# Four-layer decoder on one core: two stage boundaries of layer 2 interleaved, and layer-norm statistics moved

## The reference

```
x = x + tanh(g_ffn[1])   * L1_ffn(layernorm(x))        # entmax gates, two rank-64 maps, gelu
x = x + tanh(g_xattn[2]) * L2_xattn(layernorm(x), ctx)
    Sim = hc@w1 + hq@w2 + (hc*w3)@hq.T + b             # hc: tokens, hq: 64 context rows
    hq_hat = softmax(Sim, 2) @ hq
    hc_bar = softmax(max(Sim, 2), 1) @ hc              # one row for each batch of 256 tokens
    out = [hc, hq_hat, hc*hq_hat, hc*hc_bar] @ W_qv + b_qv
x = x + tanh(g_ffn[2])   * L2_ffn(layernorm(x))        # 16 experts, top 4 by sigmoid, SiLU; one shared
x = x + tanh(g_xattn[3]) * L3_xattn(layernorm(x), ctx) # 16 heads over 64 keys
x = x + tanh(g_ffn[3])   * L3_ffn(layernorm(x))        # 8 experts, top 2, with capacity
```

## Time and profile before

| | |
|---|---|
| executions shown, median | 1265.06 us |
| the profiled execution, its span | 1268.88 us, 1266.9 us |
| PE busy | 1069.6 us, 84% of the span |
| DVE busy | 762.4 us, 60% |
| ACT busy | 476.9 us, 38% |
| POOL busy | 354.3 us, 28% |
| chain that ended last | PE 58%, issue 17%, DVE 13%, ACT 5%, DMA 4% |
| mean granted TensorE clock | 0.899 |

### The profile page before, as it was taken

How to read it: one execution, slowest core, us unless ns; L and a number is a source line. 1 busy time by engine, 2 the same in 40 slices (tenths; PEclk the granted TensorE clock), 3 DMA queues, 4 the chain that set the end, 5 groups by cost and what they waited for, 6 DMA issues and landing times.

```text
span 1266.9 us, 17786 instructions
## 1 busy us (share of the span) xinstructions
PE 1069.6 (84%) x6301; PEld 649.1 (51%) x6302; DVE 762.4 (60%) x2192; ACT 476.9 (38%) x914; POOL 354.3 (28%) x391
## 2 busy tenths in 40 slices
PE   7889999987889986997988899999898883398870
PEld 5346666655534445334774566666455442166650
DVE  2667777778856677764664555556567764443324
ACT  1445555540034442552224233432344431254523
POOL 0050000001252175201325113000426554255551
PEclk9989999995579995898998999999999995599995
DMA  7091000030000002000003345333000011400016
GB/s 176 18 324 42 1 1 1 1 83 0 0 1 1 2 1 106 1 1 1 1 1 68 69 96 106 69 68 68 1 2 29 25 35 35 186 28 32 28 37 210
DMA packets 36163, 61.90 MB, mean 49 GB/s; under 512 B 5969, under 2 KB 20408, under 8 KB 34994
## 3 DMA queue, kind: packets, MB, share of 16 engines
q1 hardware_dynamic: 31474, 52.33, 15.3%
q0 software_dynamic: 4608, 8.50, 2.1%
HBM read 40.40 MB, written 21.45 MB: 49 GB/s over the span
## 4 chain that ended last, share of the span: by engine, by line
PE 58%; issue 17%; DVE 13%; ACT 5%; DMA 4%; POOL 2%; another core or an unknown queue 1%; SPq 0%; DVEq 0%; POOLq 0%; ACTq 0%
PE bank L534 6%; PE bank L412 5%; PE bank L455 5%; PE bank L1124 5%; PE bank L1065 3%; PE bank L1135 2%; PE bank L441 2%; PE bank L392 2%; PE bank L597 2%; PE bank L448 2%; PE bank L1079 2%; DVE nmax L1915 2%; DMA big_a<-gates 2%; PE bank L553 2%; ACT att L1278 2%
## 5 line engine op out<-in xcount | busy, mean ns | idle before, releaser
L1065 PE MATMUL bank<-big_b 128*128 128x512 f32 x288 | 140.4, 613 | 0.0
L1915 DVE TENSOR_REDUCE nmax<-bank 128x16 f32<-128x1024 f32 x64 | 78.4, 1225 | 62.4 <-PE bank L540 38.0
L1585 POOL TENSOR_SCALAR xn<-xw,mean,rstd 128x128 f32<-128x128 f32 x64 | 51.3, 810 | 189.1 <-PE bank L515 95.6
L1745 POOL DMA_INDIRECT expert_outs<-big_a,big_b x80 | 77.9, 974 | 76.4 <-DVE big_a L2534 54.3
L1461 ACT ACTIVATE att<-bank 128x512 f32<-128x512 f32 (+1 forms) x72 | 43.0, 597 | 141.6 <-PE bank L1065 141.2
L1079 PEld LDWEIGHTS bank<-big_b,att 128*128 128x128 f32 (+1 forms) x576 | 73.1, 192 | 33.5 <-issue 17.4
L2423 DVE TENSOR_TENSOR att<-att,bank 128x512 f32<-128x512 f32 (+1 forms) x72 | 49.2, 684 | 63.8 <-PE bank L1079 59.4
L1079 PE MATMUL bank<-big_b,att 128*128 128x128 f32 (+1 forms) x576 | 78.3, 279 | 5.8 <-DVE xw L1858 4.0
L1732 POOL DMA_INDIRECT expert_rows<-xw,big_b x64 | 63.3, 989 | 68.7 <-DVEq L2013 52.0
L1858 DVE SCALAR_TENSOR_TENSOR xw<-bank,tg,xw 128x128 f32<-128x128 f32 (+3 forms) x80 | 43.0, 537 | 65.4 <-PE bank L455 47.0
L1278 ACT ACTIVATE att<-bank 128x1024 f32<-128x1024 f32 x64 | 62.0, 1021 | 44.0 <-PE bank L576 44.0
(11 more groups left out here) (409 smaller groups left out, 2235.4 us busy)
## 6 DMA issues: line engine op xcount, KB each, us to landing
big_a<-gates SPq DMA_DIRECT2D x14, 1024.0 KB, 9.7
expert_rows<-big_b SPq DMA_DIRECT2D x1, 5240.0 KB, 20.3
expert_outs<-big_b SPq DMA_DIRECT2D x1, 4096.0 KB, 32.5
big_a<-expert_outs SPq DMA_DIRECT2D x6, 512.0 KB, 7.8
big_a<-expert_rows SPq DMA_DIRECT2D x1, 2620.0 KB, 14.4
xw<-in_x SPq DMA_DIRECT2D x1, 2048.0 KB, 11.0
big_a<-in_mask SPq DMA_DIRECT2D x2, 1024.0 KB, 12.4
big_b<-in_w_in SPq DMA_DIRECT2D x1, 2048.0 KB, 8.3
```

The source lines that it names most:

```text
L1065: mm = nc.tensor.matmul(bank[2 * (n % 3) + k][:, :], w13[:, k, c * 128:(c + 1) * 128], xnT_all[:, g * GW:(g + 1) * GW], start=True, stop=True)
L1585: ins = nc.gpsimd.tensor_scalar(xn[:, b % 2, j], x[:, t], mean[:, t:t + 1], rstd[:, t:t + 1], SUB, MUL)
L1745: nc.gpsimd.indirect_dma_start(outs3, bass.IndirectOffsetOnAxis(numbers3[:, ex, i:i + 1].bitcast(u32), 0), xs[:, ex, i, 0:D], None, bounds ...
L1915: nc.vector.tensor_reduce(nmax[:, j], psum[:, 2048:3072].rearrange("p (h t) -> p h t", t=T), AX.X, MAX, negate=True).then_inc(s.free, 1)
```

## The change

PE. The features of group 0 of the similarity attention are transposed in mumoe's last turn, and its similarities stand between the two halves of that turn's second rank map. The 12 unread matmuls are gone. Layer 3's keys and gate weights move from the experts' start into turn 0 of the similarity attention. In the attention's last turn PE also does the experts' features, logits and the first two `up`. The waits for `layer_done` 4 and 5 are gone. Here is PE at the end of mumoe before (L873, L879, L888: hidden, second rank map, outputs; L1009 the unread matmuls; L936 features, L945 and L947 similarities; L956 maxima, L980 probabilities):

```diff
@@ -900,2 +900,4 @@
             gate_transposes(g + 1)
+        else:
+            features_s(0)
         hidden(g, 1)
@@ -909,2 +911,6 @@
         rank2(g, 0)
+        if last:
+            pe.wait_ge(r_g_evac, 2 * NG - 1)
+            pe.wait_ge(m.g2, 3)
+            similarities(0)
         rank2(g, 1).then_inc(r_z2, 1)
@@ -1007,32 +1011,47 @@
-    for n in range(12):
-        nc.tensor.matmul(bank[5][:, :], identb[:, :], negI[:, :], start=True, stop=True)
...
+    def turns(features2, logits2, up2):
+        for g in range(NG):
+            if g:
+                pooled_transpose(g - 1)
+                if g == 1:
+                    pe.wait_ge(keys_evac, 6)
+                outputs_attended(g - 1)
+            maxima_transposes(g)
+            if g:
+                outputs_own(g - 1)
+            else:
+                layer3_keys(0)
+                layer3_gates()
+            probability_transposes(g)
+            if g + 1 < NG:
+                features(g + 1)
+            attended(g)
+            if g == NG - 1:
+                features2(0)
+            weight_transposes(g)
+            if g == 0:
+                layer3_keys(1)
+            pooled(g)
+            if g + 1 < NG:
+                similarities(g + 1)
+        logits2(0)
+        pooled_transpose(NG - 1)
+        outputs_attended(NG - 1)
+        pe.wait_ge(m.sub, NG)
+        up2(0)
+        outputs_own(NG - 1)
+        up2(1)
+    return features, similarities, turns
+def layer3_keys(n):
+    if n:
+        pe.wait_ge(r_o_read, NG)
+    nc.tensor.matmul(bank[(5, 7)[n]][:, :], wblk[:, 0], ctxT[:, n * 512:(n + 1) * 512],
+                     start=True, stop=True).then_inc(keys_mm, 1)
...
+def layer3_gates():
+    nc.tensor.matmul(bank[4][:, 0:NE3], y[:, 0], wg3, start=True, stop=True).then_inc(keys_mm, 1)
...
+def experts2(similarity_turns):
@@ -1082,9 +1107,7 @@
-    features(0)
-    logits(0)
-    for n in range(NC2 * NG):
+    similarity_turns(features, logits, up)
+    gate_transpose(0)
+    for n in range(2, NC2 * NG):
         g, c = divmod(n, NC2)
         up(n)
-        if n == 0:
-            gate_transpose(0)
         if g + 1 < NG:
@@ -1159,11 +1182,7 @@
 pe.wait_ge(layer_done, 3)
-mumoe()
-pe.wait_ge(layer_done, 4)
 pe.wait_ge(dma_w[1], 3 * 16)
-similarity_attention()
-pe.wait_ge(layer_done, 5)
 pe.wait_ge(dma_blk, 32)
-layer3_keys()
-pe.wait_ge(keys_evac, 7)
-down2 = experts2()
 pe.wait_ge(g_built, 2 * B)
@@ -1392,2 +1411,4 @@
                     gate_evac(g + 1)
+                else:
+                    first_similar()
         if first:
@@ -1417,9 +1438,17 @@
-def similarity_attention():
+def layer3_keys(n):
+    act.wait_ge(keys_mm, (5, 7)[n])
+    nc.scalar.activation(khat[:, n * 512:(n + 1) * 512], bank[(5, 7)[n]][:, :], ACT.Identity,
+                         bias=colb[:, COL_BK:COL_BK + 1]).then_inc(keys_evac, 1)
-    def feature_evac(g):
-        act.wait_ge(m.xT, g + 1)
-        nc.scalar.copy(xnT[:, g % 2], bank[0][:, :]).then_inc(m.xT_evac, 1)
+def layer3_gates():
+    act.wait_ge(keys_mm, 6)
+    nc.scalar.copy(wg3, bank[4][:, 0:NE3]).then_inc(keys_evac, 1)
+def similar_features(g):
+    act.wait_ge(m.xT, g + 1)
+    nc.scalar.copy(xnT[:, g % 2], bank[0][:, :]).then_inc(m.xT_evac, 1)
-    feature_evac(0)
+def similarity_attention():
+    nc.scalar.activation(warm[:, 3:4], ones[0:1, 0:1], ACT.Exp)
     for g in range(NG):
@@ -1433,3 +1465,5 @@
         if g + 1 < NG:
-            feature_evac(g + 1)
+            similar_features(g + 1)
+        if g == 0:
+            layer3_keys(1)
@@ -1476,3 +1510,3 @@
         ex, i, n = chunks[q]
-        act.wait_ge(k3.root, LOAD_OF[q] + 1)
+        act.wait_ge(k3.root, LOAD_OF[q])
         for j in range(i, i + n):
@@ -1496,3 +1530,2 @@
-    norms(0)
     features(0)
@@ -1672,6 +1695,8 @@
     pool.wait_ge(stats_ready, 4)
-    pool.wait_ge(m.xn, 1)
-    for g in range(1, NG):
+    pool.wait_ge(front_sems.xT, NG)
+    for g in range(NG):
         if g > 1:
             pool.wait_ge(m.hc, g - 1)
+        if TPG * g == FIRST_SIMILAR:
+            pool.wait_ge(stats_ready, 5)
         for j in range(TPG):
@@ -1697,5 +1722,9 @@
-    pool.wait_ge(front_sems.xn, F2S["xn"] + 1)
+    pool.wait_ge(stats_ready, 6)
+    pool.wait_ge(m.hc, NG - 1)
+    norms(0)
+    pool.wait_ge(m.hc, NG)
     norms(1)
-    pool.wait_ge(keys_evac, 6)
+    pool.wait_ge(keys_evac, 7)
+    pool.wait_ge(m.o_read, NG)
     for g in range(2, NG):
@@ -1703,2 +1732,4 @@
         keys(2 * g - 3)
+        if TPG * g == FIRST_NORMED:
+            pool.wait_ge(stats_ready, 7)
         norms(g)
@@ -2058,12 +2089,3 @@
         values(0)
-        token_statistics(SETTLED, TPG)
         rest = slice(SETTLED, NT)
-        nc.vector.drain().then_inc(layer_done, 1)
-        dve.wait_ge(layer_done, 7)
-        moments_of(rest)
-        first_root(rest)
-        for _ in range(3):
-            better_root(rest)
-        nc.vector.drain().then_inc(stats_ready, 1)
-        constants()
         for b in range(B):
@@ -2071,2 +2093,4 @@
                 output(b - 1)
+            if b == B - 1:
+                slots(NB3 - 3)
             if b > 1:
@@ -2075,2 +2099,7 @@
                 maxima(b + 1, 0)
+            if b == 1:
+                dve.wait_ge(layer_done, 7)
+                moments_of(rest)
+            if b == 2:
+                constants()
             if b > 2:
@@ -2082,3 +2111,13 @@
                 split(b + 1)
-            if b > 4 and b % 2:
+            if b == 0:
+                token_statistics(SETTLED, TPG)
+                nc.vector.drain().then_inc(layer_done, 1)
+            if b == 1:
+                first_root(rest)
+                better_root(rest)
+            if b == 2:
+                better_root(rest)
+                better_root(rest)
+                nc.vector.drain().then_inc(stats_ready, 1)
+            if b > 4 and b % 2 and b < B - 1:
                 slots((b - 5) // 2)
@@ -2300,2 +2340,10 @@
         output(g - 1)
+        if g == 5:
+            step(nc.vector.drain())
+            moments_of(settled)
+            first_root(settled)
+        if g == 6:
+            better_root(settled)
+            nc.vector.drain().then_inc(stats_ready, 1)
+            step(tensor_scalar(y[:, 0], ident[:, :], -1.0 / D, None, ADD))
         if g + 1 < NG:
@@ -2303,9 +2351,10 @@
         rank2(g)
-    output(NG - 1)
+        if g == 5:
+            better_root(settled)
+            better_root(settled)
+    return output
-def similarity_attention():
-    for j in range(TPG):
-        ins = norm(xn[:, 0, j], j)
-    ins.then_inc(m.xn, 1)
+def similarity_attention(last_output):
     step(nc.vector.memset(wt, 0.0))
+    first, rest = slice(0, FIRST_NORMED), slice(FIRST_SIMILAR, NT)
@@ -2359,2 +2408,5 @@
     similarities(0)
+    last_output(NG - 1)
+    nc.vector.drain().then_inc(layer_done, 1)
+    dve.wait_ge(layer_done, 4)
     for g in range(NG):
@@ -2369,2 +2421,11 @@
             token_statistics(TPG * (g - 1), 2)
+        if g == 1:
+            moments_of(rest)
+        if g in (2, 3):
+            better_root(rest)
+        if g == 4:
+            step(nc.vector.drain())
+            moments_of(first)
+        if g in (5, 6):
+            better_root(first)
         weights_evac(g)
@@ -2374,2 +2435,14 @@
         pooled_row(g)
+        if g == 1:
+            first_root(rest)
+        if g == 2:
+            better_root(rest)
+        if g == 3:
+            nc.vector.drain().then_inc(stats_ready, 1)
+        if g == 4:
+            first_root(first)
+        if g == 5:
+            better_root(first)
+        if g == 6:
+            nc.vector.drain().then_inc(stats_ready, 1)
         if g + 1 < NG:
@@ -2439,6 +2507,11 @@
-    norms()
     route(0)
+    last_output(NG - 1)
     for n in range(LAG):
         used(n)
+        if n == 1:
+            token_statistics(TPG * (NG - 1), TPG)
+            nc.vector.drain().then_inc(layer_done, 1)
+    dve.wait_ge(layer_done, 5)
+    moments_of(rest)
     for n in range(LAG - 1):
@@ -2453,2 +2526,8 @@
             token_statistics(TPG * (g - 1), TPG)
+        if n == LAG:
+            first_root(rest)
+        if n in (LAG + 1, LAG + 2, LAG + 3):
+            better_root(rest)
+        if n == LAG + 4:
+            nc.vector.drain().then_inc(stats_ready, 1)
         if g + 1 < NG and c == (7 if g == 0 else 4):
@@ -2517,3 +2596,9 @@
         newton_root(of(slot_root), of(slot_var), of(slot_tmp), of(xs)[:, :, :, VAR])
-        stt(of(slot_shift), of(xs)[:, :, :, MEAN], -1.0, of(slot_root), MUL, MUL).then_inc(k3.root, 1)
+        if n == 0:
+            for j in range(TPG):
+                row = xs[:, 0, j, 0:D]
+                ins = tensor_scalar(row, row, xs[:, 0, j, MEAN:MEAN + 1], slot_root[:, 0, j:j + 1], SUB, MUL)
+            ins.then_inc(k3.normed, 1)
+        else:
+            stt(of(slot_shift), of(xs)[:, :, :, MEAN], -1.0, of(slot_root), MUL, MUL).then_inc(k3.root, 1)
```

85 lines of the change are left out of this document (23 added, 62 removed).

## The result

| | kernel before | changed kernel |
|---|---|---|
| executions, first chip | 1265.61 us median of 4 (1262.37 to 1266.7) | 1245.38 us median of 4 (1244.12 to 1249.65) |
| the profiled execution, its span | 1268.88 us, 1266.9 us | 1245.56 us, 1243.5 us |
| executions, second chip | 1240.19 us median of 9 (1237.56 to 1244.9) | 1220.64 us median of 5 (1217.13 to 1224.09) |
| ratio, first chip | | 0.9844, 95% interval 0.9818 to 0.987 |
| ratio, second chip | | 0.9848, 95% interval 0.982 to 0.9877 |

The change saves 1.6%, about 20 us. The forecast was 1247, the measured median is 1245.4. That the two lie so close is in part luck: the clock cost more at the first seam than the forecast allowed, the second seam's gain varies by some us from execution to execution, and some us of the medians' difference are not placed anywhere.

A forecast was written before the change was run, and what follows sets the result against it. PE was taken to bound the stages' middles, other waits the seams between. Terms 7.0 + 7.0 + 3.4 + 0.7 = 18.1 us off 1268.88, less 3.8 for a long profiled execution, gave 1247; range 1242 to 1251, with rivals 1238 to 1257.

The forecast's parts named there:

- Seam A: Mumoe to similarity attention: statistics, norm and `exp` leave the path; gain 7.0 us, between 3.4 and 10.5.
- I take a fall of about 7 us, which costs half of that: Start of the similarity attention: low clock for about 7 us costs 3.5 us, taking the gain from 10.5 to 7.0.
- The pieces of statistics: Similarity attention, turns 1 and 4: small DVE instructions ahead of what PE waits for cost 0.3 and 0.4 us.
- The step on mumoe's last turn: Features' transposes and similarities added on PE delay the last statistics by 1.6 us; the sum starts at 583.4, not 590.15.
- Seam B: Similarity attention to experts: gates' DMA 7.5 us earlier, less 0.5 for Newton pieces; gain 7.0 us, between 4.0 and 8.7.
- The DMA chain, of unchanged length: Start of the experts: gates out and broadcasts in take as long as before, so the DMA's 7.5 us lead carries on.
- Seam C: Start of layer 3: first maxima ahead of the statistics end PE's 3.04 us wait; gain 3.4 us, between 2.4 and 4.2.
- Seam D: Experts of layer 3: first chunk's norm on DVE, not ACT; gain 0.7 us, between 0.3 and 0.8.
- Rival (2): Clock falls as long as before after the first seam; sum 14.5 us, 1250.6, with every low end 1255; chance 0.25.
- Rivals (1): Clock stays up at the seams; gain 24.2 us, 1240.9; chance 0.10.
- (3): Slower: clock, once down, stays down through all turns of the similarity attention; 10.0 us slower, 1275; chance 0.04.
- (4): No change: DVE pieces give the gain back; 1262 to 1266 us; chance 0.04.

The follow-up runs named there:

- e3_newton: Changed kernel with the Newton steps of the experts' statistics moved into DVE's wait for the second group of broadcasts; median 1247.14 us, ratio 0.9848 to the kernel before.

## Why the prediction was right, and where it was not

**Seam A**, forecast 7.0, measured 5.3. The first half held: the sum was to start 6.75 earlier and starts 7.03 earlier, since it starts 1.36 us behind the place where the last statistics ended before, against the 1.6 forecast: the last turn of mumoe grew by 1.17 (its last residual comes 7.87 after M and came 6.70), and the sum waits 0.19. PE's waits in turn 0 were estimated at 0.8, 1.5 and 1.5; they are none, 1.83 and 0.94. The failing step is "I take a fall of about 7 us, which costs half of that". The fall lasted 13.7 us. From the sum to the maxima of turn 1 it took 10.78 and not the 8.5 of full clock, and turn 1 took 11.64, as slow as before (11.66). At full clock the forecast was 10.5, and the two orders in which the clock held or came back soon gained 11.4 (84.12 − 72.73, unread matmuls) and 10.6 (84.12 − 73.54, no interleaving), so the rest of the working stands within 0.9. The pieces of statistics, forecast 0.7, took 0.9: 0.64 from the maxima of turn 2 to those of turn 7 (42.21 us, before 41.57), and 0.3 in turn 1, which takes 8.61 at full clock.

12 unread matmuls put into turn 0's waits kept the clock at 1.00 from 580 to 600 in both executions, so the clock held with the waits filled, and the last `attended` came 6.1 us earlier, though the total gained nothing that shows. That is not the price of removing the 12 old ones: those stood ahead of the norm, the clock fell behind them all the same, and no run puts them back there. The Trainium skill, page "TensorE: Matmul & The Clock Gate", section "What's actually happening", has the rule that was weighed in the prediction, that activity releases the throttle. The runs agree in that the clock held where the waits were filled. They do not agree that activity is enough to end a fall: once fallen, the clock stayed down for 13.7 us in which PE was busy throughout, and there the measurement decides.

The step on mumoe's last turn was right in size and missed its point. It priced the interleaved work at 1.6 us and took the earlier sum for the gain; that the same work, left behind the outputs, fills PE's wait for the sum was not seen. The interleaving brought 0.8 us at the sum, and with the longer fall behind it the last `attended` comes 5.3 later than without it.

**Seam B**, forecast 7.0, measured 7.3 (13.85 us between the third gates' DMAs of the two profiles less 6.53 between the last `attended`), and 5.5 in the second profile of the changed kernel. In the eight profiles with the same code in this seam and no fall in the last turn it is 3.5 to 8.1, 6.1 in the mean; that 7.3 lies so near to 7.0 is luck. The DMA was to come 7.5 earlier and came 7.9 earlier. "The DMA chain, of unchanged length" was not exact: it varies from 14.0 to 17.3 by execution. `route(0)` was not late, as said: its last instruction starts at 658.81, and the gates' transpose waits until 661.68 behind `up`. PE's wait for the second gates grew from 2.44 to 4.58; how much of it is the pieces on DVE, forecast 0.5, is open, between 0.4 and some 2 us (`e3_newton`). The work put inside the last turn, priced here with all the rest, is 1.2 us of the DMA's 7.9.

**Seam C**, forecast 3.4, measured 3.98 (11.80 to 7.82), and 3.89 when undone; the 0.4 taken off for pieces did not show. **Seam D**, forecast 0.7, measured 0.87, and 0.7 to 0.9 when undone. `slots(5)`: forecast 0, none shown.

Together 5.3 + 7.3 + 4.0 + 0.9 = 17.5 us in the profile, against 18.1 forecast. With 3.5 to 8.1 for seam B it is 13.7 to 18.3. The medians lie 20.2 apart, with an interval of 16.5 to 23 us from the ratio's, so the sum is inside it, at its lower end, and 2.7 us of the difference are not placed. The 3.8 us taken off for the long profile of before stand on one execution; what the two profiles differ by outside the change, 1.3 + 1.9 + 0.6 + 3.5 − 1.2, is some 6 us and so larger. Rival (2), a fall as long as before, came nearest to the length of the fall at seam A (17 us, the forecast 7, measured 13.7); in what the seam gained the two are about as far off (3.4 and 7.0, measured 5.3). It counted the whole way from the sum to the maxima of turn 1 as 12.2 us, and it took 10.78, since `attended` was still nearly at full clock (1.38). Rivals (1), (3) and (4) did not happen; in turns 2 to 7 the clock was 1.00.

## What to carry to other kernels

In this kernel, work of the next stage did better in the engine's wait than ahead of it. Moved ahead, it brought 0.8 us and left the engine idle later, and the lower clock behind that idle time cost 6.1; look for where the engine will wait after the change, and leave work for it there. A term for the clock needs both orders priced, and its stretch can be read back by counting from a point ahead of the change. Two executions of one kernel differ by some us in places the change never touched, and only such a count keeps that out of the result.

## What had not been expected of the hardware

- With PE busy in 5.00 of 5 us, three windows in a row, the clock stayed at 0.50 to 0.57 (585 to 600, changed kernel). Being busy did not end that stretch at once; stretches at this seam lasted 3.4, 6.8, 10.2, 13.7 and 17.1 us.
- The clock fell once, for some 10 us, in a turn where PE had been busy in 4.08 of 5 us, at a place where the 13 other profiles show none.
- The stretch at a given seam mostly has the same length for the same order of work: with the changed kernel's order, six of seven profiles agree within 0.04 us at the last `attended`, and the seventh is 3.3 earlier.
- DVE's product that waits for the second group of broadcasts, the same bytes each time, started between 14.0 and 17.3 us after the gates' own DMA was issued.
- A second chip of the same kind ran each of the three kernels timed on both 2% faster, about 16 of some 25 us at layer 3's routing with its indirect DMAs.
